# Decay attention in one loop of 128 steps: the diagonal blocks take another place in the order of TensorE, VectorE and ScalarE

## The reference

```
q = x @ W_q;  k = x @ W_k;  v = x @ W_v
latent_kv = (k + v) @ W_down_kv
k_rec = (latent_kv @ W_up_k)...;  v_rec = (latent_kv @ W_up_v)...
scores = jnp.einsum('bhqd,bhkd->bhqk', qh, k_rec) / math.sqrt(d)
decay = jnp.exp(-LAMBDA_DECAY * jnp.abs(t[:, None] - t[None, :]))
scores = scores * decay[None, None, :, :]
attn = jax.nn.softmax(scores, axis=-1)
out = jnp.einsum('bhqk,bhkd->bhqd', attn, v_rec)
```

## Time and profile before

| | |
|---|---|
| median of 3 runs | 1193.95 us (1192.58 to 1194.89) |
| profiled execution, its own time | 1193.0 us |
| span in its trace | 1191.2 us |
| the loop of 128 steps in it | about 308 to 705 us |
| busy share of the span: TensorE, VectorE, ScalarE, GpSimd | 88%, 64%, 54%, 16% |
| mean granted TensorE clock | 0.958 |

### The profile page before, as it was taken

How to read it: one execution, slowest core, us unless ns; L and a number is a source line. 1 busy time by engine, 2 the same in 40 slices (tenths; PEclk the granted TensorE clock), 3 DMA queues, 4 the chain that set the end, 5 groups by cost and what they waited for, 6 DMA issues and landing times.

```text
span 1191.2 us, 14247 instructions
## 1 busy us (share of the span) xinstructions
PE 1049.5 (88%) x5224; PEld 399.8 (34%) x5224; DVE 765.8 (64%) x1234; ACT 645.8 (54%) x1098; POOL 185.8 (16%) x107
## 2 busy tenths in 40 slices
PE   5899998986988888888888999998899757999998
PEld 2233333331233332333333333443333222344343
DVE  2677236279999999989998222015599998983200
ACT  4687455262477777777777653326753464413321
POOL 0222800033000000000000000000064213460000
PEclk9899999996799999999999989999899978999999
DMA  7000000069623032130000000000000000000000
GB/s 255 1 1 1 0 0 1 31 236 290 114 37 61 3 60 42 21 61 4 7 8 3 6 1 0 1 0 1 0 1 0 1 0 1 1 0 1 18 1 18
DMA packets 31194, 38.24 MB, mean 32 GB/s; under 512 B 7964, under 2 KB 22300, under 8 KB 30744
## 3 DMA queue, kind: packets, MB, share of 16 engines
q1 hardware_dynamic: 31128, 37.37, 12.5%
HBM read 23.23 MB, written 13.86 MB: 31 GB/s over the span
## 4 chain that ended last, share of the span: by engine, by line
PE 54%; ACT 15%; DVE 10%; issue 3%; DMA 1%; SPq 1%; DVEq 0%; POOL 0%; ACTq 0%
PE PS L1430 17%; PE PS L1030 11%; ACT arena L1039 8%; PE PS L1014 5%; DVE ffn L926 3%; ACT arena L1045 3%; PE PS L1419 2%; PE PS L1420 2%; PE PS L1439 2%; PE PS L916 1%; PE PS L1071 1%; DVE arena L1653 1%; PE PS L1605 1%; PE PS L981 1%; PE PS L1595 1%
## 5 line engine op out<-in xcount | busy, mean ns | idle before, releaser
L926 DVE CUSTOM_DVE_ANT_0 ffn<-PS,XP 128x1024 bf16<-128x1024 f32 x256 | 304.4, 1217 | 29.8 <-PE PS L916 29.8
L1039 ACT ACTIVATE arena<-PS 128x384 f32<-128x384 f32 (+1 forms) x512 | 252.8, 550 | 126.5 <-PE PS L1014 125.4
L916 PE MATMUL PS<-arena 48*128 48x512 bf16 (+3 forms) x704 | 195.4, 344 | 12.4 <-DMA arena<-scr 7.5
L1014 PE MATMUL PS<-arena 50*128 50x512 bf16 (+3 forms) x640 | 157.7, 322 | 18.4 <-ACT arena L1039 11.6
L1030 PE MATMUL PS<-arena 128*32 128x512 f32 (+1 forms) x1280 | 138.3, 521 | 17.8 <-ACT arena L1045 17.6
L1458 ACT ACTIVATE arena<-PS,w_scl 128x512 f32<-128x512 f32 x64 | 43.7, 687 | 157.6 <-PE PS L1430 157.5
L1430 PE MATMUL PS<-arena,w_h1T 128*128 128x512 f32 x256 | 117.8, 606 | 11.3 <-DVE arena L1468 6.6
L1430 PE MATMUL PS<-arena,w_h2T 128*128 128x512 f32 x256 | 114.9, 594 | 0.0
L1014 PEld LDWEIGHTS PS<-arena 50*128 50x128 bf16 x640 | 44.7, 94 | 153.4 <-ACT arena L1039 140.8
L1653 DVE TENSOR_TENSOR_SCAN arena<-arena 128x512 f32<-128x512 f32 x64 | 83.1, 1299 | 0.1
L1682 POOL TENSOR_TENSOR arena<-arena 128x512 f32<-128x512 f32 x32 | 58.6, 1832 | 154.8 <-DVE arena L1661 154.8
(11 more groups left out here) (219 smaller groups left out, 1538.9 us busy)
## 6 DMA issues: line engine op xcount, KB each, us to landing
arena<-scr SPq DMA_DIRECT2D x64, 192.0 KB, 5.8
scr<-arena SPq DMA_DIRECT2D x16, 384.0 KB, 5.3
scr<-arena SPq DMA_DIRECT2D x16, 256.0 KB, 4.7
scr<-arena SPq DMA_DIRECT2D x16, 128.0 KB, 3.1
XP<-xT SPq DMA_DIRECT2D x1, 1024.0 KB, 4.8
w_h1T<-h1T SPq DMA_DIRECT2D x1, 1024.0 KB, 8.1
w_h2T<-h2T SPq DMA_DIRECT2D x1, 1024.0 KB, 8.4
arena<-MH SPq DMA_DIRECT2D x64, 4.0 KB, 1.7
```

The lines of the kernel that those rows point to most:

```text
L916: mm = t.matmul(PS[:, bank, k0 - lo:k1 - lo], packed(m, g, v, slice(q * P, (q + 1) * P), KP), packed(m, g, 2 + v, slice(k0, k1), KP), star ...
L926: v.tensor_tensor_reduce(JUNK[:, u % 2, :], PS[:, bank:bank + 2, :].rearrange("p a b -> p (a b)"), STRIP[:, at:at + S], 1.0, -3.0e38, ALU. ...
L1014: mm = t.matmul(PS[:, score_bank(T, i), at:at + b_ - a_], packed(n, g, 2 + v, slice(kt * P, (kt + 1) * P), KP + MROWS), packed(n, g, v, sl ...
L1039: nc.scalar.activation(PT[:, T % 2, score_head(T, i), a0_:a1_], PS[:, score_bank(T, i), a0_:a1_], ACT.Exp).then_inc(s_free, 1)
```

## The change

Nothing is computed otherwise, and no instruction is added or taken away; three lists are written in another order.

```
             if T >= RING:
                 scores_pe(t, T, 2)
                 scores_pe(t, T, 3)
+            if turn is None:
+                diag(HEADS[0:2])
+                diag(HEADS[2:4])
...
             if T > 0:
                 pv_pe(t, T - 1)
+            if turn is not None:
+                maxima_pe(t, turn)
             if T < RING:
                 scores_pe(t, T, 2)
             unit(1, 0)
-            if turn is None:
-                diag(HEADS[0:2])
-            else:
-                maxima_pe(t, turn)
             if T < RING:
                 scores_pe(t, T, 3)
             unit(1, 1)
             if turn is not None:
                 diag(HEADS[0:2])
-            diag(HEADS[2:4])
+                diag(HEADS[2:4])
```

```
-            for i in range(GH):
-                exp_act(a, T, i)
+            exp_act(a, T, 0)
+            exp_act(a, T, 1)
+            if is_diag(T):
+                diag_exp_act(a, T)
+            exp_act(a, T, 2)
+            exp_act(a, T, 3)
...
-            if is_diag(T):
-                diag_exp_act(a, T)
```

```
+        fix_dve(v, 0)
         for T in range(NSTEP):
...
-            if is_diag(T):
-                fix_dve(v, T)
             if T in TURNS:
                 both_sides_dve(v, TURNS[T])
             if u < NUNIT:
                 unit_dve(v, u)
             if T in TURNS:
                 maxima_dve(v, TURNS[T])
+            elif not is_diag(T) and T + 1 < NSTEP:
+                fix_dve(v, T + 1)
             if u < NUNIT:
                 unit_dve(v, u + 1)
+            if T in TURNS:
+                fix_dve(v, T + 1)
```

More of the change, by code:

```diff
@@ L1151, in a1_pe @@
                 unit(1, 0)
[L1152 to L1155, removed]
                 if T < RING:
```

## The result

The changed kernel takes 1265.3 us (median of 4 runs, 1248.9 to 1283.7), before 1194.4; the ratio is 1.050, 95% interval 1.042 to 1.058. The runs of the changed kernel lie far apart, and the two slowest of them are left out of the ratio; a second series of it gave 1262.8 and 1.053 (1.046 to 1.061; the slowest left out), so the scatter is the kernel's own. The direction was right, the size wasn't: 1225 was forecast, and 1265 lies outside 1205 to 1246.

What follows compares the result with a forecast made beforehand. It took a circle through TensorE and ScalarE, no engine being full, to bound the loop. Even, odd, half_out and turn period changes summed to +31.1 us, 1193.95 + 31.1 = 1225.0; range 1205 to 1246.

Steps and rivals of the forecast that it cites:

- The circle: Loop through TensorE and ScalarE: value product, scores 2, exponents 2 and 3, scores 1, unit half; ordinary period 2.88 us.
- the block's 0.55: Diagonal block on TensorE, both pairs one behind the other, occupies 0.55 us in front of the value product.
- the 0.26 for the exponent: Even steps: taking the diagonal exponent off the circle lets the value product start at 2.62, not 2.88: 0.26 at most.
- the turn's wait for the fix: At a turn the value product stands behind L994, which waits for VectorE's fix: period 4.57 against 3.43, +1.14.
- The sum at full clock: All period changes of steps 0 to 115 added: +31.1 us, making 1224.1 on the profiled execution.
- The bounds 1214 to 1238: Span given 0.60 chance: odd-step and turn terms each a fourth off, plus the tail's 2 us.
- The rival of the short wait: Block's second pair follows the first without a gap: block 0.22, even steps 2.84, odd 3.05, total 1207; chance 0.17.
- The other side: Block and fix hide in TensorE's idle time during exponents 2 and 3, only gains stay: 1176; chance 0.10.
- the rival that named it: Granted clock falls at the turns, one to two steps at 1.1 each, 16 to 33 us: 1241 to 1258; chance 0.13.
- Tail and last turn: From step 116 moved blocks displace equal work: 0, within 2 us either way; last turn (115) +0.8.

Runs made afterwards that it cites:

- e8: Changed kernel with L994 and the diagonal exponent early, but L981 behind the value product in odd steps and the turn in the old order: 1194.5 us, ratio 1.001.
- e5: Changed kernel plus two zero-weight matmuls of 256 columns at each turn, in front of L981 and of L994, where TensorE waits: 1227.3 us, ratio 1.028.
- e4: Changed kernel with turns in the old order; in most other steps the block's first pair before scores 1, the second behind the unit half: 1191.5 us, ratio 0.998.
- e2: Kernel before the change, with the diagonal block ahead of the value product only in the step after each turn: 1224.5 us, ratio 1.024.
- e9: Changed kernel, turn left as changed; in ordinary steps the block's first pair stands before scores 1, the second behind the unit half: 1215.9 us, ratio 1.019.
- e7: Changed kernel with VectorE's fix at a turn moved ahead of its second unit: 1271.1 us, ratio 1.066.
- e1: Changed kernel, but in the step after each turn the diagonal block and its exponent keep their old places: 1211.8 us, ratio 1.016.
- e3: Changed kernel plus two zero-weight matmuls of 512 columns at each turn, in front of L981 and of L994: 1238.6 us, ratio 1.038.

## Why the prediction was wrong in size, point by point

- **The circle** of value product, exponents 2 and 3 and scores 1 was right, and so was where things lie on it. Right too: the block's 0.55 in front of a full-array matmul (0.55 at 531.16, 534.44 and 541.53), the 0.26 for the exponent (e8: 2.62), the turn's wait for the fix (4.47 against 4.57, inside its bounds of 4.43 and 4.67).
- **The sum at full clock** was right: 1224.1 against about 1223 from both traces, and 1227 by e5, where the clock stays up but its turns take 4.56 and the loop leaves the lower level only at 328. With the measured periods in place of the forecast ones (+0.19, -0.25, -0.26, +0.40, +1.04, last turn +0.8) it would be +30.7 instead of +31.1. The bounds 1214 to 1238 given for it don't follow from what they name: a fourth of 16.8 and of 16.0 and the 2 us are 10, so 1215 to 1235.
- **The rival of the short wait** (1207) was wrong: even and odd steps take 3.07 and 3.28, not 2.84 and 3.05. The second pair's weights are loaded 0.33 behind the first pair (531.49 against 531.16), and e4 gets 0.34 back by splitting the pairs.
- **The other side** (1176) was wrong by the reason given: the idle time of TensorE lies ahead of scores 1, and the block behind them. Where e4 puts a pair into that idle time, the gain appears.
- **The step that failed** is the clock: the sum put it at nothing, and the rival that named it had too small a chance and too small a price. Measured are 61 and 39 us. The mechanism was named: falls at the turns, where one value product is 4.5 from the next. I gave it 0.13, because the clock was 1.00 over the whole loop before. That row speaks for turns of 3.43, not of 4.47; rows 9 had a fall with TensorE busy 2.13 of 3.00 us, and a turn went from 2.42 of 3.00 to 1.83. The mean over long stretches hid the question, which was what a turn's few us look like. Those few us would have raised the chance, not settled it: 1.97 of 3.00 in the kernel before had brought no fall.
- **The size:** I took one to two steps of +1.1 for each fall, 16 to 33 us in all. Measured is +1.49 for a step at the lower level (4.66 against 3.18, the means of the two periods), since in the changed kernel the block, too, takes longer in front of the value product (0.80 instead of 0.55, 405.57 to 406.37). What weighs more is that stretches last up to all eight steps, and that the one at the loop's start can last longer too: 191 us in one trace, 122 in the other, 61 and 39 us of time. The one row of before on which the price rested, 311.98 to 315.95, was a period in which the clock rose again, and nothing in it told how long a fall would last.
- **Tail and last turn** were right. The last turn takes 6.01 (747.06 to 753.07) against 5.23 before (655.52 to 660.75), +0.78 for +0.8. From there to the end of the span pass 528.8 us against 530.5, within the 2 us either way.

Open is what decides how long the clock stays down. In e2 (ordinary steps as before) it came back within 7 us, in e9 (split pairs) within 14, in the changed kernel and in e7 after 3 to 41. This goes with how much stands in front of each value product at the lower level, but e7, with shorter turns than the changed kernel, had no shorter stretches. The distance from turn to turn differs between these kernels too (26.1 at full clock in the changed kernel, 27.2 with a short fall in it; 25.9 in e7, 25.0 in e2, 24.4 in e9), and the runs don't separate the two. The eight long stretches (31 to 34 us) of the first trace of the changed kernel and of e7 all ended within four us of the start of the next turn, behind the period that has no block in front of its value product; of the three stretches over 10 us in the second trace of the changed kernel one did. Open, too, is why the stretch at the loop's start ended at 315 to 328 in twelve traces, and at 351 and 352 in the first of the changed kernel and in e7.

## What to carry to other kernels

Find the circle that sets the period and price every place on it: a block that was free where TensorE waited for ScalarE cost 0.40 to 0.45 a period in front of the value product, and about 0.11 once its two dependent halves were put on either side of other work. Before an edit lengthens a wait of TensorE, look at the stretch of a few us around it, not at the mean of the loop: two waits that had been apart fell into one period, and the clock took more (39 and 61 us in the two traces) than the waits themselves (14 x 1.04, 15 us). If such a wait can't be avoided, work for TensorE within it, even useless work, can be the cheaper way: e5 is 38 us faster than the changed kernel.

## What the runs showed of the hardware that I had not expected

- The granted clock stayed down for 31 to 34 us at a time in a loop in which TensorE was busy over 90% by its records (30.61 of 32.00 in e7): busy time at the lower level says little, since each matmul lasts longer. The Trainium skill ("TensorE: Matmul & The Clock Gate", HAM oscillation) has a kernel whose clock goes up and down with its waits for data. The runs agree that waits bring the fall (e1, e5: without the two in one period no turn in the loop has one). But the waits here are short: 0.43 and 0.62 at the turn shown, and none in front of a fall in the first trace is longer than 0.67 as the profile lists them.
- A matmul of 512 float32 columns on all rows, put between matmuls that use half the rows each, keeps TensorE for 1.06 (541.53 to 542.59 in e3) and not for the 0.86 by which such matmuls follow each other elsewhere (starts at 262.15, 263.01 and 263.87 in the trace of before). At 0.86, too, it would have been longer than the turn's waits of 0.43 and 0.62.
- Runs of one kernel differ by 3% (1249 to 1289), with a mean granted clock from 0.932 to 0.882; the order of instructions is the same in all of them.
